# Four cross-attention layers on one core: the maxima's turn moved to the projections' bank, maxima in strictly alternating banks, and two quarters of the values joined with the denominators

## What is computed

```python
# layer 0: 16 heads of 64, a bias on four key columns, no norm
# layers 1 to 3: 16 query heads of 32, 4 key/value heads, RMS norm
xn = rmsnorm(x, norm_w)
q = (xn @ wq).reshape(B, T, N_HEADS, HEAD_DIM)
k = (cond @ wk).reshape(B, S, N_KV_HEADS, HEAD_DIM)
v = (cond @ wv).reshape(B, S, N_KV_HEADS, HEAD_DIM)
scores = einsum('btgrd,bsgd->bgrts', qg, k) * scale
attn = softmax(scores)
out = einsum('bgrts,bsgd->btgrd', attn, v)
return residual + out @ wo
```

## Time and profile before

| | us |
|---|---|
| median of the runs | 4432.54 |
| profiled execution | 4432.37 |
| its span | 4430.5 |
| PE busy | 4158.9 (94% of the span) |
| DVE busy | 2515.7 (57%) |
| ACT busy | 2077.2 (47%) |
| POOL busy | 2008.8 (45%) |

### The profile page before, as it was taken

How to read it: one execution, slowest core, us unless ns; L and a number is a source line. 1 busy time by engine, 2 the same in 40 slices (tenths; PEclk the granted TensorE clock), 3 DMA queues, 4 the chain that set the end, 5 groups by cost and what they waited for, 6 DMA issues and landing times.

```text
span 4430.5 us, 62098 instructions
## 1 busy us (share of the span) xinstructions
PE 4158.9 (94%) x19496; PEld 2654.1 (60%) x19496; DVE 2515.7 (57%) x3453; ACT 2077.2 (47%) x2648; POOL 2008.8 (45%) x1072
## 2 busy tenths in 40 slices
PE   9999999988999999999788999998999999899999
PEld 7888888874665566555444554554555555454555
DVE  3122200016556655566577777777777777777775
ACT  2111211114344444444265666665666666656665
POOL 0000000004555555565256665655666566656665
PEclk9999999998999999999899999999999999999999
DMA  5333522235444554454322322323222333223322
GB/s 182 132 128 136 160 87 82 93 96 138 119 127 124 130 132 118 126 136 130 96 81 69 81 78 81 90 81 88 75 81 77 89 90 91 73 75 81 85 74 66
DMA packets 316045, 451.72 MB, mean 102 GB/s; under 512 B 45176, under 2 KB 117368, under 8 KB 315832
## 3 DMA queue, kind: packets, MB, share of 16 engines
q1 hardware_dynamic: 315832, 448.86, 36.0%
HBM read 217.72 MB, written 102.77 MB: 72 GB/s over the span
## 4 chain that ended last, share of the span: by engine, by line
PE 37%; DVE 5%; ACT 5%; issue 4%; SPq 0%; POOL 0%; DVEq 0%; DMA 0%; ACTq 0%
PE a_ps L2017 9%; PE a_ps L2063 7%; PE a_ps L2049 6%; PE a_ps L2006 6%; PE a_ps L2086 5%; DVE a_max_cols L1885 3%; ACT a_q_ops L1769 2%; PE a_ps L2074 2%; PE a_ps L2079 2%; ACT a_probs L1778 2%; PE a_ps L2040 1%; PE a_ps L1992 1%; DVE a_stage L1904 1%; DVE x_lo L1895 1%; DVE wq_lo L1862 0%
## 5 line engine op out<-in xcount | busy, mean ns | idle before, releaser
L1885 DVE TENSOR_REDUCE a_max_cols<-a_ps 128x1 f32<-128x512 f32 x1536 | 1022.5, 672 | 421.2 <-PE a_ps L2017 415.4
L1778 ACT ACTIVATE a_probs<-a_ps 128x1024 f32<-128x1024 f32 x768 | 784.7, 1025 | 692.9 <-PE a_ps L2049 690.6
L2017 PE MATMUL a_ps<-a_k_ops,a_q_ops 96*128 96x512 f32 x1536 | 699.9, 457 | 110.1 <-DVE a_max_cols L1885 84.2
L1687 POOL TENSOR_TENSOR a_sums<-a_probs 128x1024 f32<-128x1024 f32 x192 | 454.5, 2386 | 412.2 <-ACT a_probs L1778 412.2
L2017 PEld LDWEIGHTS a_ps<-a_k_ops,a_q_ops 96*128 96x128 f32 x1536 | 296.9, 193 | 512.2 <-DVE a_max_cols L1885 273.5
L1036 DVE TENSOR_REDUCE a_max_cols<-a_ps 128x1 f32<-128x512 f32 x522 | 346.0, 686 | 351.0 <-PE a_ps L1189 351.0
L2049 PE MATMUL a_ps<-a_q_ops,a_k_ops 128*128 128x512 f32 x1536 | 494.7, 404 | 32.7 <-issue 32.0
L1687 POOL TENSOR_TENSOR a_sums<-a_sums,a_probs 128x1024 f32<-128x1024 f32 x192 | 463.9, 2436 | 19.8 <-ACT a_probs L1778 19.8
L803 POOL MEMSET a_ident<- 128x128 f32 x1 | 0.2, 204 | 976.5 <-issue 976.5
L2063 PE MATMUL a_ps<-a_probs,a_v 128*32 128x512 f32 x3072 | 428.6, 631 | 0.0
L303 DVE TENSOR_TENSOR cp_c_lo<-cp_raw,cp_c_hi 128x1024 fp32r<-128x1024 f32 x64 | 78.4, 1225 | 528.2 <-ACT cp_c_hi L247 528.1
(11 more groups left out here) (131 smaller groups left out, 7424.6 us busy)
## 6 DMA issues: line engine op xcount, KB each, us to landing
a_k_ops<-k_scratch SPq DMA_DIRECT2D x201, 256.0 KB, 4.0
a_q_ops<-a_qn_hi SPq DMA_DIRECT2D x768, 64.0 KB, 2.0
k_scratch<-cp_out SPq DMA_DIRECT2D x88, 512.0 KB, 2.8
a_q_ops<-a_qn_hi SPq DMA_DIRECT2D x268, 128.0 KB, 2.3
cp_raw<-in_ctx_t SPq DMA_DIRECT2D x64, 512.0 KB, 4.1
x_raw<-out_t SPq DMA_DIRECT2D x25, 1024.0 KB, 5.7
a_q_ops<-a_qn_lo SPq DMA_DIRECT2D x384, 64.0 KB, 2.0
a_x_res<-out_t SPq DMA_DIRECT2D x92, 256.0 KB, 2.9
```

What stands on the lines that cost most here:

```text
L1687: pool.tensor_tensor(sums[:, hp], (probs if n < H else sums)[:, hp], probs[:, n], ALU.add)\
L1778: act.activation(probs[:, n], ps[:, 2 * (n % 2):2 * (n % 2) + 2, :], ACT.Exp).then_inc(exped, 1)
L1885: dve.tensor_reduce(max_cols[:, t % 2, col:col + 1], bank(b), AX.X, ALU.max, negate=True)\
L2017: pe.matmul(bank(b), q_ops[0:SHIFT, s, h, q * P:(q + 1) * P], k_ops[0:SHIFT, s, :], start=True, stop=True).then_inc(smax, 1)
```

## The change

1. The turn goes to bank 7 instead of bank 5. It waits until DVE has added the tile's projected block, and the denominators, the next to use bank 7, wait until ACT has copied both halves of the turned maxima.
2. Maxima alternate strictly between banks 4 and 5. M13 and M14 no longer wait for the reduction of the maximum directly before them, and M15 no longer for ACT; each waits for the one two before.
3. A tile's program is cut in two: `second_part` (from O1 or M11 on) is emitted ahead of the next tile's `first_part`. The loop's edge so lies between P3 and O1 of a tile t = 3, where it was between M15 and S0.
4. O2 moves behind M0 of the next tile, where O3 and D follow it. O1 moves behind M11 and stands directly ahead of T. P2 and P3 move forward, behind M10; for t = 3 all four P stand there.
5. Q0 and Q1 are taken apart, with M3 between them.
6. DVE: `add_result` comes before M11's reduction (was before M15's), R3 after it (was before), and each split of x or part of the mean square one maximum later or where it was. `rest_wo` follows M2 (was M6), and on ACT `round_wo` comes before the tile's second exponential (was after the fourth).

The order on PE is now S0 M0 O2 O3 D M1 S1 M2 Q0 M3 Q1 S2 M4 Q2 M5 Q3 S3 M6 O0 M7 S4 M8 P0 M9 P1 S5 M10 P2 P3 M11 O1 T S6 M12 M13 S7 M14 M15.

```diff
-    OUTB, FB, TURNB = 6, 7, 5
+    OUTB, FB = 6, 7
-    MAXB = (4, 5, 4, 5, 4, 5, 4, 5, 4, 5, 4, 5, 4, 4, 4, 5)
+        def max_bank(i):
+            return 4 + i % 2
...
             def maximum(it, t, i):
...
-                    if i == 15:
-                        pe.wait_ge(shifted, 2 * (tile_no(it, t) + 2))
-                    else:
-                        pe.wait_ge(reduced, no if i in (13, 14) else no - 1)
-                    one_maximum(*at(it, t_m), n, MAXB[i])
+                    pe.wait_ge(reduced, no - 1)
+                    one_maximum(*at(it, t_m), n, max_bank(i))
             def turn(it, t):
...
-                    pe.wait_ge(reduced, (g - 1) * M + LEAD + 12)
+                pe.wait_ge(reduced, (g + 1) * M)
+                if there(it, t - LAG - 1):
+                    pe.wait_ge(added, g - LAG)
+                else:
+                    pe.wait_ge(q_taken, g + AHEAD)
+                    pe.wait_ge(ms_step, 2 * MS if t > 0 else 2 * MS + 1)
...
             def denominators(it, t):
...
-                wait(pe, added, g - LAG + 1)
+                if there(it, t + 1):
+                    pe.wait_ge(shifted, 2 * (g + 2))
+                else:
+                    pe.wait_ge(added, g - LAG + 1)
...
+            def first_part(it, t, par):
+                scores(it, t, 0)
+                maximum(it, t, 0)
+                outputs(*at(it, t - 1), KT - 2, par if t > 0 else 1 - par)
+                outputs(*at(it, t - 1), KT - 1, par if t > 0 else 1 - par)
+                denominators(*at(it, t - 1))
+                maximum(it, t, 1)
+                scores(it, t, 1)
+                maximum(it, t, 2)
+                project_q(*at(it, t + AHEAD), range(1))
+                maximum(it, t, 3)
+                project_q(*at(it, t + AHEAD), range(1, 2))
...
+                if t < T - 1:
+                    project_out(it, t, par, 0)
+                    maximum(it, t, 9)
+                    project_out(it, t, par, 1)
+                    scores(it, t, 5)
+                    maximum(it, t, 10)
+                    project_out(it, t, par, 2)
+                    project_out(it, t, par, 3)
+                else:
+                    maximum(it, t, 9)
+                    scores(it, t, 5)
+                    maximum(it, t, 10)
+                    for tile in range(T):
+                        project_out(it, t, par, tile)
+            def second_part(it, t, par):
+                if t == T - 1:
+                    outputs(it, t, 1, par)
+                    maximum(it, t, 11)
+                else:
+                    maximum(it, t, 11)
+                    outputs(it, t, 1, par)
+                turn(*at(it, t + 1))
+                scores(it, t, 6)
+                maximum(it, t, 12)
+                maximum(it, t, 13)
+                scores(it, t, 7)
+                maximum(it, t, 14)
+                maximum(it, t, 15)
+            def batch(it, par):
+                for t in range(T):
+                    if there(it, t - 1):
+                        second_part(*at(it, t - 1), par if t > 0 else 1 - par)
+                    first_part(it, t, par)
...
+                if t < T - 1 and there(it, t - LAG):
+                    add_result(it, t)
+            def second_part(it, t, par):
+                if t == T - 1 and there(it, t - LAG):
+                    add_result(it, t)
+                maximum(it, t, 11)
+                reciprocal(*at(it, t - 1), 3)
...
+                maximum(it, t, 12)
+                if t == T - 1 and there(it, 2 * T):
+                    invert_mean_square(it + 2, 0)
+                if t == 0 and there(it, T):
+                    split_x(it + 1, 0)
+                maximum(it, t, 13)
+                if t == 0 and there(it, T):
+                    split_x(it + 1, 1)
+                maximum(it, t, 14)
+                if t == T - 1 and there(it, 2 * T):
+                    invert_mean_square(it + 2, 1)
+                if t == 0 and there(it, T):
+                    split_x(it + 1, 2)
+                    where(dve, it, par, B - 1, lambda: rest_wq(it // B + 1))
+                maximum(it, t, 15)
```

More of the change, by code:

```diff
@@ L1794, in round_output @@
                 act.activation(a_hi[:, par, t, :], stage[:, t % 2, :], ACT.Copy).then_inc(o_hi, 1)
+            def first_part(it, t, par):
+                exponential(it, t, 0)
+                if there(it, t - 2):
+                    round_output(*at(it, t - 2), par if t >= 2 else 1 - par)
+                if there(it, t - 1):
+                    take_outputs(*at(it, t - 1))
+                    take_denominators(*at(it, t - 1))
+                if t == 1:
+                    where(act, it, par, 1, lambda: round_wo(it // B))
+                exponential(it, t, 1)
+                if isinstance(it, int) and it == 0 and t == 0:
+                    squares(1)
+                if t == 1 and there(it, T):
+                    act.wait_ge(q_taken, (it + 1) * T)
+                    inv_rms(it + 1)
+                exponential(it, t, 2)
+                exponential(it, t, 3)
+                if there(it, t + AHEAD):
+                    round_q(*at(it, t + AHEAD))
+                exponential(it, t, 4)
+                if t == 0 and there(it, T):
+                    round_x(it + 1, 0)
+                if t == 2 and there(it, 2 * T):
+                    squares(it + 2)
+                exponential(it, t, 5)
@@ L1796, in batch @@
+            def second_part(it, t, par):
+                if t == 0 and there(it, T):
+                    round_x(it + 1, 1)
+                    where(act, it, par, B - 1, lambda: round_wq(it // B + 1))
+                exponential(it, t, 6)
+                if there(it, t + 1):
+                    shift(*at(it, t + 1), 0)
+                exponential(it, t, 7)
+                if there(it, t + 1):
+                    shift(*at(it, t + 1), 1)
             def batch(it, par):
                 for t in range(T):
-                    exponential(it, t, 0)
@@ L2167, in _ @@
             pairs(pe, batch)
+            second_part(N - 1, T - 1, 1)
+            outputs(N - 1, T - 1, KT - 2, 1)
             outputs(N - 1, T - 1, KT - 1, 1)
```

170 lines of the change are left out of this document (64 added, 106 removed).

## The result

The changed kernel takes 4365.7 us (median of four runs, 4351.1 to 4371.3) against 4432.6 for the kernel before beside it: 0.9843 of its time, 95% interval 0.9818 to 0.9867, 67 us less. 4390 was forecast, with 4350 to 4434 as the range. The profiled execution took 4367.3 with a span of 4365.4. PE is busy for 4119.0 us, 94% as before; DVE for 2462.1 instead of 2515.7.

What follows compares the result with a forecast made beforehand. PE, busy 94% of the span, was taken to bound the kernel through its order and small gaps. Terms 21.5 - 14 + 14 + 19.5 + 2 = 43 us off 4432.4 gave 4389, stated as 4390; range 4350 to 4434.

Steps and rivals of the forecast that it cites:

- Plain tiles: Tiles without special work: 20.76 us each, 0.5 less than 21.27; some 43 of them, 21.5 us won.
- The gain is nearly all from the joined groups: In plain tiles, joining O2 to O3 saves PE 0.32 us a tile; the removed waits nearly all come back.
- 1.3 of waits given against 1.2 come back: PE's waits in a plain tile: 1.3 us removed at M3, M14 and M15, 1.2 returning at the tile's new end.
- t = 3: Tiles t = 3 take 22.9 us, 0.6 more than 22.26; 22 tiles, 14 us lost.
- the 1.79 of waits at the end: End of tiles t = 3: DVE reduces M12 to M14 later, so O2 starts at 6.5 us for 4.74, 1.79 late.
- Loop's edge: Instruction refill moves from M15|S0 to P3|O1, hidden in neither place: 0, from -10 to +10 us for ten edges.
- t = 0: Tiles t = 0, with splits of x one maximum later: 22.4 us where it was 23.06, 22 times, 14 us won.
- their low end: Splits of x on DVE at t = 0 take 0.67 us each without POOL; for all, tile 21.4, 36 us won.
- Output weights: Three tiles that split the output weights: 25.2 us for 32.31; taken as 6.5 won each, 19.5 us.
- Clock: Falls of PE's granted clock over the stage: 0 net, with ends at 15 falls less (-23 us) or 15 more.
- Rival A: Many falls of the clock go and half the splits of x are at their low end: 4355 us; chance 0.22.
- the 15 falls less: PE's clock falls 15 times less, as t = 0's end wait becomes three smaller pieces: 23 us less.

Runs made afterwards that it cites:

- run 1: Changed kernel with O2 moved back behind M14 of its own tile, alone again: 4280.9 us, ratio 0.9655 to the kernel before.
- run 7: Kernel before the change with only M3 placed between Q0 and Q1: 4394.6 us, ratio 0.9913 to the kernel before.
- run 6: Changed kernel with the maxima's old table of banks, M12, M13 and M14 sharing bank 4: 4396.4 us, ratio 0.9919 to the kernel before.
- run 3: Changed kernel with R3 and the mean square's first part right behind M10's reduction in tiles t = 3: 4338.7 us, ratio 0.9788 to the kernel before.
- run 9: Changed kernel with O2 alone behind M14, and P0 to P3 and O1 in tiles t = 3 ordered as in other tiles: 4270.3 us, ratio 0.9635.
- run 4: Changed kernel with the cut of the tile undone, so the loop's edge lies between M15 and S0 again: 4387.8 us, ratio 0.9900.

## Why the prediction fell within its range, and where its reason was wrong

The result lies within the range, but outside the 4370 to 4412 that had a chance of 0.53, and with 67 us instead of 43. What was right are the tiles worked out row by row; what was wrong are one reason and one term.

- **Plain tiles: right in size.** 20.76 forecast, 20.84 and 20.92 measured, 18 us instead of 21.5. The starts of M14, S0, O2 and the denominators came out within 0.13.
- **"The gain is nearly all from the joined groups": wrong.** The prediction netted 1.3 of waits given against 1.2 come back, and was left with the joins. That is bookkeeping and not cause. With O2 apart the tile is 20.42 (run 1), 0.42 shorter though PE loses the 0.32 of the join, so some 0.74 of the 1.2 came back because of the join. M3's 0.35 is a gain by itself (run 7), and so are the alternating banks, 0.7 (run 6). The step that failed is to credit the join with 0.32 without asking what O2 had hidden at its old place. What the turn's new bank and the places of P2, P3 and O1 in plain tiles give or take no run shows.
- **t = 3: right.** 22.9 forecast, 22.98 measured, 8 us lost on the eleven tiles without an edge. Both causes were the right ones: the places of R3 and the mean square's first part (run 3), and M7 to M9 without P0 between (run 9). But the 1.79 of waits at the end, too, is mostly what the join uncovered: with O2 apart the tile is 22.17.
- **Loop's edge: mis-sized.** 0 forecast, "nothing hides it in either place". The ten tiles became 9 us shorter where their like became 7 longer, 16 us in all, beyond the bound of 10 (and there are nine edges, not ten). Something does hide it in the new place: PE's gaps are 23.8 in all for 32.0, and DVE's reciprocal and its late reductions now lie beside them (run 4 puts the edge back: +21, 12 of it waits).
- **t = 0: 21 us won instead of 14.** Without a fall it is 22.02 where 22.4 was forecast; the splits took 0.79, 1.15 and 0.68, nearer to their low end. The Trainium skill, "SBUF — State Buffer", § Who interferes with whom, has a VectorE instruction with two SBUF inputs and a GpSimd one that reads SBUF shut each other out for a whole instruction. The runs agree: 0.68 clear of POOL, 2.25 behind its sum.
- **Output weights: 22 instead of 19.5.** One of the three tiles had no fall and took 23.61, the other two 25.2, the forecast. The four subtractions took 2.50 (2.4 forecast) where 6.78 stood:

```profile
2316.23 2.18 ACT L1743 ACTIVATE wq_hi<-a_w_raw 128x512 fp32r<-128x512 f32 x4
2318.44 2.50 DVE L1872 TENSOR_TENSOR wq_lo<-a_w_raw,wq_hi 128x512 fp32r<-128x512 f32 x4 [0.92 <-ACT wq_hi L1743]
2322.40 0.50 PE L2038 MATMUL a_ps<-a_k_ops,a_q_ops 96*128 96x512 f32 x1 [2.58 <-DVE a_max_cols L1895]
```

- **Clock: 0 forecast, nearly so.** Low time 136.5 before and 105.8 after; all but 7 of the difference is the weights' 23.9 (already in their term). At t = 0 14 of the 20 tiles had a fall before and 15 after. That the granted clock swings when PE idles briefly between its groups, as the Trainium skill says of one kernel in "TensorE: Matmul & The Clock Gate", § A second HAM failure mode: psum-queue depth-cycling, does not hold for plain tiles in any run: 0 low time in all 39, with one idle time of 0.3 in most of them before and after and with 0.79 and 0.31 in run 6. At t = 0 it could be said of the changed kernel (0.80 and 0.70 close together), where the falls went with the first wait (run 1), but not of run 6, with three waits and no fall.
- **The sum.** In the stage 65.3 us went where 43 were forecast: 3.7 less in plain tiles, 1.2 more lost at t = 3, then 16.3 more at the edges, 7.1 at t = 0, 2.4 at the weights and 1.4 in the first and last tiles. Nearly three quarters of the miss is one term, the edge. Rival A's 4355 was nearer than the forecast. Of its two reasons the splits near their low end came true, the 15 falls less did not: at t = 0 there is one more.

## What to carry to other kernels

A group of PE that stands alone costs its switches (0.3 here), but it is also cover for the engines that PE waits for next. Before two groups are joined, follow what each of them hid. And list gains and new waits by edit and not by kind: two edits whose sums cancel can be one that pays and one that costs, and one run for each tells them apart. The gap at a loop's edge is priced with what the other engines still have to do beside it, not by its own length alone.
